# A fused attention and mixture-of-experts block: new order at the head of a loop body, at the passage to the experts, and at the gather of an expert tile

## What is computed

```python
h = layernorm(x) * (1 + ca) + sa
x = x + ga * attention(h)          # linear attention, 16 heads of 16, its output normed and projected
h = layernorm(x) * (1 + cb) + sb
scores = sigmoid(h @ gate_w + bias)            # 8 experts
top_scores, top_idx = top_k(scores, 2)         # each token goes to two experts
top_scores = top_scores / (sum(top_scores) + 1e-6)
eo = gelu(h @ up_w[e] + up_b[e]) @ down_w[e] + down_b[e]     # 256 -> 1024 -> 256
combined = sum over the two experts of 0.1 * top_scores * eo
shared = (gelu(h @ sw_up + sb_up) @ sw_down + sb_down) * 0.1
out = shared + combined
out = out / (max(abs(out), axis=-1) + 1e-6)
return x + gb * out
```

## Time and profile before

| what | us |
|---|---|
| median of three runs | 974.72 |
| the three runs | 974.68, 974.72, 981.07 |
| profiled execution, device time | 978.45 |
| its span | 976.7 |
| PE busy in it | 862.2 (88%) |
| DVE busy | 633.5 (65%) |
| ACT busy | 476.0 (49%) |
| POOL busy | 408.0 (42%) |

### The profile page before, as it was taken

How to read it: one execution, slowest core, us unless ns; L and a number is a source line. 1 busy time by engine, 2 the same in 40 slices (tenths; PEclk the granted TensorE clock), 3 DMA queues, 4 the chain that set the end, 5 groups by cost and what they waited for, 6 DMA issues and landing times. The chain is left out here.

```text
span 976.7 us, 21393 instructions
## 1 busy us (share of the span) xinstructions
PE 862.2 (88%) x5989; PEld 790.6 (81%) x5990; DVE 633.5 (65%) x1668; ACT 476.0 (49%) x880; POOL 408.0 (42%) x407
## 2 busy tenths in 40 slices
PE   6899999799989889899938999998999999999980
PEld 5688788688777778778737999988999999999980
DVE  5778776557677676687663766557666666666651
ACT  3665555333435435435425655546555555555530
POOL 3723600110432422423330356554656566655554
PEclk9899999779999999999978999999999999999995
DMA  8120000620321321312276233352433343344442
GB/s 275 61 87 1 1 1 0 174 42 2 111 75 37 111 73 39 110 48 64 90 266 196 58 91 89 84 165 64 93 83 90 85 89 82 80 84 77 90 81 39
DMA packets 68608, 82.78 MB, mean 85 GB/s; under 512 B 23217, under 2 KB 56970, under 8 KB 68400
## 3 DMA queue, kind: packets, MB, share of 16 engines
q0 software_dynamic: 25792, 39.39, 17.4%
q1 hardware_dynamic: 41392, 41.12, 13.5%
q10 hardware_dynamic: 1344, 1.31, 0.4%
HBM read 45.44 MB, written 41.55 MB: 89 GB/s over the span
## 5 line engine op out<-in xcount | busy, mean ns | idle before, releaser
L1724 PE MATMUL psUp<-eT,wup 128*128 128x256 f32 x1632 | 204.8, 285 | 11.5 <-issue 6.7
L1724 PEld LDWEIGHTS psUp<-eT,wup 128*128 128x128 f32 x1632 | 198.6, 193 | 16.9 <-issue 16.5
L1746 PE MATMUL psE<-wdn,gTh 128*128 128x256 f32 x1088 | 198.1, 285 | 0.0
L1746 PEld LDWEIGHTS psE<-wdn,gTh 128*128 128x128 f32 x1088 | 168.7, 192 | 0.0
L1746 PE MATMUL psE<-wdn,gTl 128*128 128x256 f32 x544 | 153.4, 282 | 0.0
L1981 POOL DMA_INDIRECT out<-fin,oidx x68 | 108.9, 1602 | 23.5 <-issue 17.1
L1785 ACT ACTIVATE gu<-psUp,ubias 128x256 f32<-128x256 f32 x272 | 113.3, 468 | 10.5 <-PE psUp L1724 6.2
L1804 ACT ACTIVATE ys<-yc,meta 128x256 f32<-128x256 f32 x68 | 30.9, 502 | 176.3 <-DVE yc L1869 137.5
L1849 DVE TENSOR_TENSOR gTl<-gu,gTh 128x512 fp32r<-128x512 f32 x136 | 93.7, 689 | 32.9 <-ACT gTh L1790 26.8
L1971 POOL DMA_INDIRECT shared_part<-ys,widx x68 | 71.0, 1044 | 91.5 <-ACT ys L1804 50.1
L1173 ACT ACTIVATE gf<-psU,sbu 128x512 f32<-128x512 f32 x64 | 44.1, 689 | 132.7 <-PE psU L1088 128.5
(11 more groups left out here) (279 smaller groups left out, 1408.7 us busy)
## 6 DMA issues: line engine op xcount, KB each, us to landing
hin<-expert_in SPq DMA_DIRECT2D x36, 256.0 KB
X<-in_L_attn_x SPq DMA_DIRECT2D x8, 512.0 KB, 7.8
X<-bo_row POOLq DMA_DIRECT2D x8, 512.0 KB, 5.6
shared_part<-prow SPq DMA_DIRECT2D x8, 512.0 KB, 8.3
out<-X SPq DMA_DIRECT2D x8, 512.0 KB
shared_part<-sh SPq DMA_DIRECT2D x7, 512.0 KB
raw_up<-in_L_ffn_up_w SPq DMA_DIRECT2D x3, 1024.0 KB
raw_dn<-in_L_ffn_down_w SPq DMA_DIRECT2D x3, 1024.0 KB, 9.3
```

The lines of the kernel that those rows point to most:

```text
L1724: mm = nc.tensor.matmul(psU[:, c, (m % 2) * TR:(m % 2 + 1) * TR], wup[s][:, a, k, m * P:(m + 1) * P], eT[:, u, b, k], start=(n == 0), stop ...
L1746: mm = nc.tensor.matmul(psE[:, u, h * C:(h + 1) * C], (gTh, gTl)[a][:, u, m, h * P:(h + 1) * P], wdn[s][:, b, m], start=(n == 0), stop=(n ...
```

## The change

It has four parts.

1. **In every body** DVE and PE take another order. `out_read` is parted in two (`out_read`, `out_stats`), `gate_copy` comes between them, the second `outs` comes ahead of `turn_gate`; `shared_read` moves from the end of a body to the head of the next; `place` moves ahead of `low_h`; `norms_inverse` moves behind `low_h`.
2. **In body 8** ACT does the sigmoid ahead of all gelus, DVE does `choose` ahead of `low_g(2)` and `place` behind it, PE does `rank` ahead of `up(4)`, and the tables are made in three pieces between `low_g`. A fourth table, `vtab`, is made.
3. **At the passage** SP stores the last x first, writes two padding tiles ahead of the weights and three behind, ACT writes the other three between gelus, and SP loads `hin` and `meta` for the first tiles inside the second stage, ahead of the barrier. `hin` and `meta` lie in the memory of x for that. DVE splits only the up weights there; the low half of the down weights comes in the third stage, behind its first `low`.
4. **In the third stage** the gather of tile j waits for the write of tile j - 2, and for the write of tile j - 1 only at the first tile of an expert: the number it waits for is read from `vtab`, which POOL loads into a register for every tile from 3 on.

```diff
+    def pad(eng, e):
+        row = entry(eng, padt, e, E * REG - TR)
+        eng.dma_start(hs[bass.ds(row, TR), :].rearrange("(h p) c -> p h c", p=P),
+                      prow[:].unsqueeze(1).broadcast_to([P, 2, ROW])).then_inc(pad_st, 16)
...
                 chunk(0)
+                if att_on:
+                    outs(1)
                 if ffn_on:
                     turn_gate()
                 chunk(1)
-                if att_on:
-                    outs(1)
...
                 chunk(3)
+                if not att_on:
+                    rank()
                 if ffn_on:
                     up(4)
...
+                if not att_on:
+                    score()
+                    for m in range(MK):
+                        gelu(m)
+                        if 4 <= m < 4 + E - SP_PADS:
+                            act.wait_ge(tab_ok, 1)
+                            pad(act, SP_PADS + m - 4)
+                    split_hi(act, 0, 0)
+                    return
...
+                out_read(0)
                 if ffn_on:
                     gate_copy()
+                out_stats(0)
+                out_read(1)
+                if ffn_on:
                     gate_read()
                 low_g(0)
+                if ffn_on and later(f, 1):
+                    shared_read(f - 1)
+                out_stats(1)
                 low_g(1)
...
+                x_norm()
+                low_g(7)
+                if ffn_on:
+                    place()
+                low_h(0)
+                low_h(1)
                 if isinstance(g, int) and g in (1, 2):
                     norms_inverse(*((3, 5), (5, NG))[g - 1])
-                low_g(7)
-                if att_on:
-                    low_h(0)
-                    low_h(1)
-                if ffn_on and not tail:
-                    place()
...
-                if ffn_on:
-                    shared_read()
...
+                link(nc.vector.tensor_reduce(tabf[:, 1], gej[:], AX.X, ALU.add))
+                link(nc.vector.tensor_scalar(tabf[:, 1], tabf[:, 1], 1.0, 2.0 * 16, ALU.min, ALU.mult))
+                nc.vector.tensor_tensor(vtab[:], tabf[:, 1], io_v[:, 0:ETL], ALU.add)
...
+            sp.wait_ge(x_ev, 2 * NG)
+            sp.dma_start(xr_v[:, TG * (NG - 1):NT, :], X[:, TG * (NG - 1):NT, :]).then_inc(x_st, 16)
+            sp.wait_ge(tab_ok, 1)
+            pad(sp, 0)
+            pad(sp, 1)
             sp.wait_ge(tab_ok, 2)
             weights(sp, entry(sp, etab, 0, E - 1))
...
+            for e in range(2, SP_PADS):
+                pad(sp, e)
+            sp.wait_ge(zero_st, 16 * NG)
             sp.wait_ge(x_st, 16 * NG)
-            sp.wait_ge(zero_st, 16 * NG)
+            sp.wait_ge(scat, 16 * TG * TOPK * NG)
+            sp.wait_ge(tab_ok, 3)
+            sp.wait_ge(pad_st, 16 * E)
+            load_rows(sp, entry(sp, rtab, 0, E * REG - TR), 0)
+            load_rows(sp, entry(sp, rtab, 1, E * REG - TR), 1)
+            load_tails(sp, entry(sp, rtab, 0, E * REG - TR), 0)
...
             low(0, 0)
+            split_lo(dve, 0, 0, (1,))
...
-                if later(j, 1):
+                if later(j, 2):
+                    wait(pool, w_st[u], 32 * i)
+                if later(j, 3):
+                    landed = pool.value_load(vtab[0:1, bass.ds(j, 1)], min_val=32, max_val=16 * ETL)
+                    wait(pool, w_st[1 - u], landed)
+                elif later(j, 1):
                     wait(pool, w_st[1 - u], 32 * i + 32 * u)
```

More of the change, by code:

```diff
@@ L39 @@
 BIG = 65536
+SP_PADS = 5
 META = 16
@@ L132, in adaln_block @@
     ntab = keep("ntab", [P, ETL], I32)
+    vtab = keep("vtab", [P, ETL], I32)
     ubias = keep("ubias", [P, E * MK], F32)
@@ L1135, in body @@
                     down(2)
-                if not att_on:
-                    rank()
                 if att_on:
@@ L1360, in place, with shared_read @@
                     nc.vector.sem_inc(pos_ok, 1)
-                def shared_read():
+                def shared_read(f):
                     dve.wait_ge(d_mm, MK * f + MK)
@@ L1370, in shared_read @@
                                                        ALU.mult, ALU.add).then_inc(sh_ev, 1)
-                tail = not att_on
-                if att_on:
-                    out_read(0)
+                if not att_on:
+                    gate_copy()
+                    gate_read()
+                    shared_read(f - 1)
+                    best()
+                    low_g(0)
+                    low_g(1)
+                    choose()
+                    low_g(2)
+                    place()
+                    low_g(3)
+                    dve.wait_ge(rt_dve, ROUTE * NG)
+                    table_experts()
+                    low_g(4)
+                    low_g(5)
+                    table_slots()
+                    low_g(6)
+                    table_rows()
+                    low_g(7)
+                    shared_read(f)
+                    split_lo(dve, 0, 0, (0,))
+                    return
+                out_read(0)
                 if ffn_on:
                     gate_copy()
+                out_stats(0)
+                out_read(1)
+                if ffn_on:
                     gate_read()
                 low_g(0)
-                if att_on:
-                    out_read(1)
+                if ffn_on and later(f, 1):
+                    shared_read(f - 1)
+                out_stats(1)
                 low_g(1)
@@ L1385, in body @@
                     norm_read(3, NG)
-                if att_on:
-                    out_norm()
+                out_norm()
                 low_g(2)
-                if att_on:
-                    low_z(0)
-                    low_z(1)
+                low_z(0)
+                low_z(1)
                 if first:
@@ L1607, in adaln_block @@
      ) = [sem(n) for n in names]
-    h_in = [sem(f"h_in{i}") for i in range(2)]
     g_in = [sem(f"g_in{i}") for i in range(2)]
@@ L1611, in adaln_block @@
     o_st = [sem(f"o_st{i}") for i in range(2)]
-    m_in = [sem(f"m_in{i}") for i in range(2)]
     MC = MK // 2
@@ L1654, in rows @@
                     wait(sp, ht_mm, j - 1)
-                sp.dma_start(hin[:, u], hs[bass.ds(row, TR), 0:C].rearrange("(h p) c -> p h c", p=P)
-                             ).then_inc(h_in[u], 16)
+                load_rows(sp, row, u)
             def ahead(j):
```

67 lines of the change are left out of this document (26 added, 41 removed).

## The result

| | before | after |
|---|---|---|
| median beside each other, us | 976.11 | 1023.41 |
| lowest and highest | 974.68, 981.07 | 1021.14, 1025.87 |
| ratio | | 1.0476 (1.0426 to 1.0525) |
| profiled execution | 978.45 | 1021.14 |

What follows compares the result with a forecast made beforehand. PE, busy 88%, was taken to be held by a ring through POOL's queue in the bodies, the passage and POOL's waits; gains 19 + 11 + 1.5 + 2.8 = 34.3 take 974.72 to 940.4 us, range 930 to 954.

Steps and rivals of the forecast that it cites:

- POOL gets 2.2 us back for each 0.6: Third stage: per tile, dropping POOL's wait returns 2.2 us against 0.6 for loading a table entry, so the loads cost nothing.
- the bounds, 0 to 4.3 and 1.5 to 3.5: Third stage: limits on the gain at the gather around tile 10, and on the gain behind the last matmuls.
- the slower one: Bodies: late `place` delays `low_h` and each `gate`, 41.3 us a body, 981.5 us; among the 0.03 for within 1%.
- 2.8 forecast: End of third stage: the last gather's wait of 3.8 us goes, 0.6 comes in; gain taken as 2.8 us.
- the 1.5 forecast: Third stage around tile 10: the gather goes out 2.2 us sooner, behind the next expert's weights; gain taken as 1.5 us.
- The six bodies were to be 206.5: Second stage: six intervals of `turn_z`, 225.5 us before, come to the ring's length; gain taken as 19 us.
- Nothing is late in their place: Bodies: with `low_h` and a wait out of the ring, 34.6 instead of 36.6 us, `rstd`'s input still comes in time.
- PE's order: Rival in the bodies: new waits at the head bring each to 36.0 us, gain 9.5, time 950; chance 0.22 for 947 to 955.
- forecast 11: Body 8 and passage: PE starts the third stage at 503.5 instead of 514.50 us, a gain of 11, bounds 7 and 13.
- The DMA-bound rival: Passage: bound by DMA, not issue; `hin` goes out at 502.5, gain 7.5 instead of 11, time 944; chance 0.15.
- The limit I set (34): Passage: the prediction is wrong if `hin`'s load is issued later than 34 us after the last `gate` begins (before, 44).
- a small chance for code loading: Loop's branch: a new stall of code loading puts the time between 955 and 965 us; chance 0.05.

Runs made afterwards that it cites:

- e2: Kernel before with only the table `vtab` and the new gather wait (part 4) added: 1017.85 us, ratio 1.0515.
- e5: The kernel before, unchanged, run and profiled again: 970.40 us.
- e1: Changed kernel with part 4 undone: every gather again waits until the writes of the tile ahead have landed: 948.57 us, ratio 0.9795.
- e14: Changed kernel, table included, with POOL issuing the fifth of a body's eight scatters only when the first four have landed: 944.72 us, ratio 0.9824.
- e16: The changed kernel itself, run once more: 934.96 us, ratio 0.9720.
- e17: Changed kernel with the pause between the fourth and fifth scatter of a body, repeated beside the changed kernel: 944.39 us, ratio 0.9817.
- e9: Changed kernel with the table's wait only from tile 32 on and the old gather wait at the tiles before: 960.56 us, ratio 0.9827.
- set 5: Runs beside the kernel before (961.51 us): the changed kernel again, it with paused scatters, and it with the old gather wait; ratios 0.9720, 0.9817, 0.9693.
- e18: Changed kernel with the old gather wait at every tile (the kernel of e1), run again: 932.47 us, ratio 0.9693.
- sets 4 and 5: The last two groups of runs, each beside the kernel before (961.62 and 961.51 us); six versions of the changed kernel took 932.47 to 944.72 us.
- set 2: Kernel before again, it with part 1 alone, and two versions of the changed kernel, beside the kernel before at 967.15 us; ratios 0.9802 to 1.0568.
- e10: Kernel of e1 (old gather wait), with the fifth of a body's eight scatters waiting until the first four have landed: 957.00 us, ratio 0.9785.
- set 3: Four versions of the changed kernel with altered waits or padding, beside the kernel before at 977.48 us; ratios 0.9785 to 0.9931.
- e6: Kernel before with part 1 alone, the new order in the bodies: 954.25 us, ratio 0.9863.
- e7: Kernel of e1 (old gather wait), with `best` behind `out_norm` on DVE instead of ahead of it: 948.62 us, ratio 0.9802.
- e12: Kernel of e1 (old gather wait), with all eight padding tiles on SP's queue instead of three on ACT's: 962.08 us, ratio 0.9848.
- e4: Changed kernel, with POOL waiting before a tile's two `out` DMAs until the next tile's gathers have landed: 961.21 us, ratio 0.9898.
- e8: Changed kernel with `out` written without adding to what stands there (`compute_op=ALU.add` left out): 1025.00 us, ratio 1.0568.

## Why the prediction was wrong

**Part 4, the step that failed.** "Before the last tiles POOL's loads cost nothing: POOL gets 2.2 us back for each 0.6." I costed the removed pause as POOL's own time, and took it for harmless to issue six DMAs in a row; the bounds, 0 to 4.3 and 1.5 to 3.5, held no loss. In its place the runs showed a loss: the third stage became 58.4 us longer, part 4 alone makes it 46.0 us longer (e2, 502.4, beside e5 of the next set, 456.4), and taking part 4 out brings it back to 457.1 (e1). The wait that I priced at 0.6 against 2.2 us of POOL had kept `out` apart from the writes. None of the rivals was this: the slower one put the loss at the `gate` of the bodies, and that did not come. The trace of before could not show it: it has rows of six in a few tiles, but with `out` third and fourth, and PE's idle time beside the fifth and sixth of them is 0.7 us.

The gains that part 4 was to bring depend on the set, and that one of them fits the forecast is luck. The last `yc` to the end fell by 3.2 us, against 2.8 forecast. But the last `out` came 5.1 us sooner, and 1.9 were lost behind it, a term that the sum left out: between its last branch and its drain POOL stands 2.5 us in the changed kernel, e2, e14, e16 and e17, which have the table at every tile, and 0.4 in those with the old wait and in e9, which has the table at the end alone. What it stands for no run shows. In set 5 the last gather waits only 1.93 us for its write under the old wait (e18), not 3.82, the last `out` is no sooner with the table, and the loss behind it stays: 23.7 us to the end (e16) against 21.1 (e18). Beside tile 10 the interval went from 16.5 (e5) to 12.7 us (e2), more than the 1.5 forecast, and from 13.1 (e18) to 12.0 (e16) in set 5.

**Part 1: the mechanism held, the size hung on the same thing.** `place`, scatters and `rstd` came as forecast. The six bodies were to be 206.5; without a pause they are 203.2 to 203.5 in sets 4 and 5, where the kernel before was not profiled, and 209.5 to 222.0 in the others. In set 2 the gain is 11.5 us, not 19. The sum left out one term: gelus and logits late beside the scatters, and with them `best`, which stands ahead of `out_norm`. "Nothing is late in their place, since `rstd`'s input has some 3 us to spare" looked at one of the two things that `out_norm` waits behind. e10 shows the cause: the pause alone puts it right. "PE's order" (36.0 a body) gives nearly the length of the bodies in set 3. One of its waits did come, 6.7 us of `down` for `shared_read` in the changed kernel, but it is gone in e16 with the same order, so the order alone doesn't make it. No `gate` came late.

**Parts 2 and 3: forecast 11, measured 8.3, and inside a set 6.6 (e2, e1) and 6.9 (e6, e7).** The DMA-bound rival (7.5) came nearest. Counted from the last `gate`, I had DVE done at 33.3 us and `hin` issued at 31.6; in the changed kernel DVE was done at 34.8, and `hin` went out at 35.2, so both were later than I took them, and `hin` came last. It stood behind the padding, which lands last: the DMA share is 1.00, 0.98 and 1.05 in the three stretches of 4 us from 478 on. The limit I set (34) is passed in every run with parts 2 and 3, with 34.4 to 35.3 us. The Trainium skill, page "DMA: Bandwidth & Descriptors", section "Issuing engines are not separate DMA queues", says that several issuing engines save sequencer time only; e12 agrees: three tiles fewer on ACT, and a passage of 38.4 us against 38.3 in e9 of the same set.

**The whole.** Even where nothing stalls PE, the changed kernel gains 26.6 us (e16, 961.51 to 934.96) and not 34.3. Without part 4 it gains 29.0 (e18).

**What stays open.** What outside the kernel decides whether POOL's issues hold PE: all runs of a set that could show it do, or none does. The gaps in the semaphore records go with it, but every timed execution has its span and clock on record, and none without recording stands beside them, so whether the recording has a part in the stalls was not tried. By what path POOL's issues hold PE: its matmuls come one in 0.74 us, and its reports to ACT and DVE late; something that POOL's issues and PE's sequencer share is a guess that no run settles. Where the limit lies: `out` as fifth and sixth behind two writes and two gathers stalls PE, a row of six that begins with `out` hardly does (e4), and the four left by the old wait don't; in the bodies a row of eight scatters makes reports late in the new order and not in the old one. The prediction has a small chance for code loading and says that the rows show it at body 5; they show a wait of PE for `gate_copy` there, and no run shows code loading.

## What to carry to other kernels

A wait on an engine that is off the path can hold something else apart, here the issues of POOL's indirect DMAs; before it is taken out, ask what then goes out back to back. Here a gap of some 2 us that parted them into rows of four or fewer in most tiles, or in every body, was enough (e1, e10); where nothing stalled, such a gap in the scatters cost 10 us over six bodies. Price a moved group of DMAs also by what runs beside it now, not only by its own engine. Measure such a change in more than one set of runs: the same two kernels gave 1.0476 and 0.9720.

## What the hardware showed

- Six indirect DMAs issued by POOL 0.30 us apart, in the order write, write, gather, gather, `out`, `out`, slow PE in mid-block to one matmul in 0.74 us beside the last two. Fewer packets and a shorter issue don't help (e8); a gap ahead of the gathers (e1, 2.3 us) or of `out` (e4, 3.5 us) does, though e4 keeps six in a row in another order; and in sets 4 and 5 the effect is absent.
- A report from PE to ACT came up to 4.7 us late beside a row of eight scatters, and on time when 2.29 us were left between the fourth and the fifth, or in sets 4 and 5 without that.
- POOL takes 1.62 us on the mean for an indirect DMA that adds to its target and 1.03 us for the same one without the addition (the changed kernel and e8, 68 each).
- Beside a memset of 128x2048 on POOL (1.86 us) an operation of DVE on 128x2 elements took 1.80 us on the mean instead of 0.25; PE's waits for DVE's `eT` came to 31.6 us in 21 places.
